# Third buffers for the split keys, packed token routing, and work moved into the attention, in a two-layer kernel on one Trainium2 core

## The reference, cut to what matters

```python
# layer 0
xn = layernorm(x)
ct_q, ct_kv = xn @ Wd_q + b, xn @ Wd_kv + b
query = heads(ct_q @ Wu_q) + heads(rope(ct_q @ Wq_r))      # 16 heads of 16
key   = heads(ct_kv @ Wu_k) + heads(rope(xn @ Wk_r))
s = softmax(query key' / scale) (ct_kv @ Wu_v) @ Wo + b
# g: 32 experts, each takes its 8 best tokens of a batch
probs = softmax(xn @ gate_w.T, over the 2048 tokens)
vals, idx = top_k(probs per expert, 8)
merged = sum_k xn[idx_k] * vals_k                          # one row per expert
o = gelu([merged, 1] @ w1) -> [.., 1] @ w2
g = zeros.at[idx].add(o * vals)                            # zero for most tokens
x = x + s * silu(g)
# layer 1: a state-space scan for s, a gated MLP for g
```

## Time and profile before

| | us |
|---|---|
| runs of the kernel before: median (lowest to highest) of 3 | 3020.09 (3019.51 to 3027.25) |
| the profiled execution, its own time | 3014.55 |
| its span, first to last instruction | 3012.9 |
| norm loop, until PE's first matmul of the key loop | 82.15 |
| key loop, until DVE's last `key_sum` | 233.5 |
| from there to the attention's first instruction | 49.5 |
| attention | 599.2 |
| scatter, from 964.3 | 47.5 |
| layer 1 | 2001.1 |

### The profile page before, as it was taken

How to read it: one execution, slowest core, us unless ns; L and a number is a source line. 1 busy time by engine, 2 the same in 40 slices (tenths; PEclk the granted TensorE clock), 3 DMA queues, 4 the chain that set the end, 5 groups by cost and what they waited for, 6 DMA issues and landing times.

```text
span 3012.9 us, 43961 instructions
## 1 busy us (share of the span) xinstructions
PE 2588.0 (86%) x13290; PEld 1488.0 (49%) x13290; DVE 2306.4 (77%) x2777; ACT 2027.6 (67%) x3268; POOL 2069.9 (69%) x650
## 2 busy tenths in 40 slices
PE   6776188888887769998999899999899899999987
PEld 2333033333333435564665555656556566566455
DVE  6577466556562269989889799898798888989995
ACT  3221146656564379878788698797787887978874
POOL 0454430000000179999999899999899999999996
PEclk9998579989998879999999999999999999999999
DMA  8335497767641123032132130321312303213210
GB/s 274 105 103 127 109 266 210 186 175 180 172 140 46 55 120 120 30 119 100 36 120 85 65 120 33 117 99 36 121 52 97 120 17 126 105 38 120 78 63 7
DMA packets 133934, 323.21 MB, mean 107 GB/s; under 512 B 13233, under 2 KB 89009, under 8 KB 117314
## 3 DMA queue, kind: packets, MB, share of 16 engines
q1 hardware_dynamic: 113186, 248.84, 26.7%
q0 software_dynamic: 19200, 70.73, 7.1%
q10 hardware_dynamic: 1312, 0.66, 0.1%
HBM read 277.12 MB, written 43.13 MB: 106 GB/s over the span
## 4 chain that ended last, share of the span: by engine, by line
PE 26%; issue 12%; POOL 12%; ACT 7%; DVE 7%; ACTq 1%; DVEq 1%; DMA 0%; POOLq 0%; SPq 0%
PE l_p_w L1995 11%; PE l_p_y L1987 6%; POOL l_st L1638 5%; PE l_p_w L2041 5%; DVE l_st L1457 4%; POOL l_st L1630 3%; PE l_p_w L2060 3%; ACT l_p_a L1716 2%; POOL keep_xg L1638 2%; DVE keep_xg L1457 1%; ACT L1791 1%; POOL l_dtu L1644 1%; ACT L1725 1%; DVE keep_xg L1466 1%; PE l_p_w L2017 1%
## 5 line engine op out<-in xcount | busy, mean ns | idle before, releaser
L1457 DVE TENSOR_TENSOR_SCAN l_st<-l_p_a,l_hl,l_st 128x512 f32<-128x512 f32 x768 | 931.6, 1265 | 112.1 <-ACT l_p_a L1716 93.0
L1638 POOL TENSOR_TENSOR l_st<-l_st,l_cs 128x2048 f32<-128x2048 f32 x192 | 868.6, 4541 | 4.1 <-ACT l_hl L1721 3.8
L1716 ACT ACTIVATE l_p_a<-l_dt,lw_a_neg 128x512 f32<-128x512 f32 x1024 | 666.1, 681 | 51.6 <-DVE keep_xg L1457 40.4
L1630 POOL TENSOR_TENSOR l_st<-l_bs,l_dtu 128x2048 f32<-128x2048 f32 x128 | 580.9, 4539 | 47.5 <-PE l_p_y L1987 44.2
L1987 PEld LDWEIGHTS l_p_y<-keep_ident,l_st 128*128 128x128 f32 x3072 | 353.8, 144 | 136.9 <-POOL l_st L1638 74.8
L1987 PE MATMUL l_p_y<-keep_ident,l_st 128*128 128x128 f32 x3072 | 382.4, 281 | 42.9 <-POOL l_st L1638 42.9
L977 ACT ACTIVATE a_pr<-a_p_s 128x512 f32<-128x512 f32 x512 | 284.8, 596 | 163.9 <-PE a_p_s L1043 145.7
L901 DVE TENSOR_REDUCE a_mpart<-a_p_m 128x1 f32<-128x512 f32 x512 | 315.2, 683 | 98.2 <-PE a_p_m L1008 96.5
L1457 DVE TENSOR_TENSOR_SCAN keep_xg<-l_p_a,l_hl,keep_xg 128x512 f32<-128x512 f32 x256 | 314.8, 1267 | 2.3 <-DVE keep_xg L1466 1.9
L1638 POOL TENSOR_TENSOR keep_xg<-keep_xg,l_cs 128x2048 f32<-128x2048 f32 x64 | 290.7, 4542 | 11.0 <-ACT l_hl L1721 11.0
L1043 PE MATMUL a_p_s<-a_qst,kx 99*128 99x256 bf16 x1024 | 206.7, 292 | 73.6 <-ACT a_pr L977 54.8
(11 more groups left out here) (225 smaller groups left out, 3920.1 us busy)
## 6 DMA issues: line engine op xcount, KB each, us to landing
a_w<-in_w_dram POOLq DMA_DIRECT2D x64, 1024.0 KB, 12.0
l_bs<-s_bc SPq DMA_DIRECT2D x64, 1024.0 KB, 4.7
l_cs<-s_bc SPq DMA_DIRECT2D x64, 1024.0 KB, 4.9
keep_share<-s_x SPq DMA_DIRECT2D x32, 512.0 KB, 4.4
s_kp<-t_kp SPq DMA_DIRECT2D x96, 128.0 KB
kx<-s_kp SPq DMA_DIRECT2D x16, 768.0 KB, 11.8
s_vp<-t_vo SPq DMA_DIRECT2D x16, 544.0 KB
a_vg<-s_vp SPq DMA_DIRECT2D x16, 544.0 KB, 11.7
```

The source lines that it names most:

```text
L1457: eng.tensor_tensor_scan(st[k % NG][:, n, :], p_a[:, n, :], st[k % NG][:, n, :], hl[:, k, n:n + 1], ALU.mult, ALU.add).then_inc(scan_ok, 1)
L1630: eng.tensor_tensor(st[n][:, :, :], bs[:, 4 * n:4 * n + 4, :], dtu[(k // NG) % 2][:, :].unsqueeze(1).broadcast_to([P, NG, TT]), ALU.mult). ...
L1638: eng.tensor_tensor(st[n][:, :, :], st[n][:, :, :], cs[:, 4 * n:4 * n + 4, :], ALU.mult).then_inc(cm_ok, 1)
L1716: eng.activation(p_a[:, n, :], dt[c % 2][:, :], ACT.Exp, scale=a_neg[:, c, m:m + 1]).then_inc(dA_ok, 1)
```

## The change

Its edits, in the order of the program:

1. Norm loop: x is no longer stored to `x1` from its buffers, and loads no longer wait for such stores. The buffers lie in `accT` now.
2. Key loop: three buffers `kp` and `vo`, two `k32`. They lie in a tensor `late` that outlives the stage and later holds the experts' `w2`.
3. The gather of `xg` is issued before `key_low(0)` instead of after `key_rest(1)`. The gather of the rotation's rows is issued in fours at tiles 4 and 6 instead of in twos at 4, 6, 8 and 9.
4. The routing steps run in tiles 0 to 12. ACT does `low(t+1)` before `high(t)`. The query parts are stored by SP at tile 13 and by ACT at tiles 13 and 14.
5. `share_of`, `rank_of` and `place` leave the loop. In the attention, `one_choice` does one column in two halves before each `take`, and the lists `rowb`, `rankb` and `rank` are loaded by SP after pass 3's loads (it issues those of passes 0 to 3 at once), and DVE waits for them in pass 1. `place` comes at the end.
6. The stage's end waits for the first two groups' keys and queries only, which it has loaded into `kst` and `q0`. The last stores of keys and values may land in the attention: SP waits for them before the loads of batch 1, POOL before its first `w2` load that overwrites them.
7. Attention: `identb` is made by ACT, and PE waits for it only at `transpose_max` of pass 0. x is copied to `x1` by eight 1 MB DMAs from DRAM to DRAM, one in each odd pass.
8. The result of an expert group uses a part of `hraw`, so `hidden_rows` waits for its store instead of `experts_out`.
9. Scatter: the eight rows' gather of `xg` is made again by POOL at its start, and DVE's first add of it waits for all eight.

On SP, in the stage's second part and at its end:

```diff
                 def keys_out(r):
-                    p = r % 2
+                    p = r % 3
...
+                def group_queries():
+                    eng.wait_ge(q_out, 16 * 6 * B)
+                    for hg in two:
+                        for g6, part in enumerate((0, 0, 0, 1, 1, 2)):
+                            eng.dma_start(q0[hg][g6 * 16:(g6 + 1) * 16, :, :].rearrange("r z t -> r (z t)"),
+                                          scr["qp"][0, hg, part * 64:(part + 1) * 64, :].rearrange("(r z) t -> r (z t)", z=4))\
+                               .then_inc(side, 16)
...
+                    if t == 13:
+                        store_queries(eng, 0)
                     if t in (10, 14):
                         group_keys((10, 14).index(t))
-                store_queries(eng, 0)
-                for p in two:
-                    eng.wait_ge(stored[p], STORES * (NT // 2))
-                for j in range(4):
-                    eng.wait_ge(x_out[j], 16 * (NT // 4))
-                eng.wait_ge(side, 16 * 9)
-                eng.wait_ge(q_out, 16 * 4 * B)
-                eng.wait_ge(q_out_g, 16 * 2 * B)
+                    if t == NT:
+                        group_queries()
+                eng.wait_ge(side, 16 * (1 + 2 * 3 + 2 * 6))
```

On DVE (`key_sum`, `values`; `high` on ACT changes as `values` does) and at the end of ACT's tile:

```diff
-                    wait(eng, r1_ok, t)
+                    wait(eng, r1_ok, t - 1)
...
-                    p = t % 2
+                    p = t % 3
                     eng.wait_ge(v_ok, t + 1)
-                    wait(eng, stored[p], t // 2 * STORES)
+                    wait(eng, stored[p], t // 3 * STORES)
...
                     if t in (13, 14):
-                        query_turned(2 * (t - 13) + 1)
-                eng.wait_ge(qsplit, 2)
-                eng.activation(qp[:, 1, :, :], qrest, ACT.Copy).then_inc(qsplit, 1)
+                        store_queries(eng, t - 12)
                 middle(NT - 1)
-                store_queries(eng, 1)
```

In the attention, on DVE, and on SP in `load`:

```diff
-                eng.tensor_copy(identb[:, :], ident[:, :]).then_inc(setup, 1)
...
+                def one_choice(g, b, hg):
+
+                    k = b * 2 + hg // 2
+                    wait(eng, shares, 6 * g)
+                    eng.tensor_copy(col[:, 0:1], gf[:, bass.ds(k, 1)])
+                    eng.tensor_copy(col[:, 1:2], vals[:, bass.ds(k, 1)]).then_inc(shares, 1)
+                    for h in two:
+                        cols = slice(h * TT, h * TT + TT)
+                        eng.wait_ge(shares, 6 * g + 2 * h + 1)
+                        if hg % 2 == 0:
+                            eng.tensor_scalar(found[:, :], rowb[:, cols], col[:, 0:1], col[:, 1:2], ALU.is_equal, ALU.mult).then_inc(shares, 1)
+                            eng.wait_ge(shares, 6 * g + 2 * h + 2)
+                            eng.tensor_tensor(share[:, cols], share[:, cols], found[:, :], ALU.add).then_inc(shares, 1)
+                        else:
+                            eng.scalar_tensor_tensor(found[:, :], rowb[:, cols], col[:, 0:1], rankb[:, cols], ALU.is_equal, ALU.mult)\
+                               .then_inc(shares, 1)
+                            eng.wait_ge(shares, 6 * g + 2 * h + 2)
+                            eng.tensor_reduce(part[:, h:h + 1], found[:, :], AX.X, ALU.max).then_inc(shares, 1)
...
-                    if not (isinstance(g, int) and g == 0):
-                        take(*prev(g, b, hg))
...
+                    if isinstance(g, int) and g == 0:
+                        return
+                    one_choice(*prev(g, b, hg))
+                    take(*prev(g, b, hg))
...
+                    if hg % 2:
+                        half = bass.ds(b * S + hg // 2 * (S // 2), S // 2)
+                        eng.dma_start(scr["x1"][half, :].rearrange("(p a) d -> p (a d)", p=P),
+                                      ins["x"][half, :].rearrange("(p a) d -> p (a d)", p=P)).then_inc(x1_out, 16)
```

In the scatter, on POOL:

```diff
+                    eng.indirect_dma_start(xg[:, k, :], None, ins["x"], bass.IndirectOffsetOnAxis(g8[:, k:k + 1], 0)).then_inc(xg_in, 16)
```

More of the change, by code:

```diff
@@ L802, in attention_stage @@
         w1 = sb("w1", [P, 4, KD, HID])
-        w2 = sb("w2", [P, 4, 8, D])
+        w2 = late[:, :].rearrange("p (j c d) -> p j c d", j=4, c=8)
+        rowb, rankb = (keep["xg"][:, 4 * i:4 * i + 4, :].rearrange("p k d -> p (k d)") for i in range(2))
+        found = sb("found", [P, TT])
+        part = sb("part", [P, 2])
+        rank, top, dup = (sb(n, [P, TOPK]) for n in ("rank", "top", "dup"))
+        col = sb("col", [P, 2])
         b1 = sb("b1", [P, NE, 8])
@@ L838, in prev, with all_stored @@
             return (g - 1, b if hg else b - 1, (hg - 1) % HG)
+        def all_stored(eng):
+            for j in range(3):
+                eng.wait_ge(stored[j], (6, 5, 5)[j] * STORES)
         def early(b, hg):
@@ L936, in step, with last @@
                         i.then_inc(hT_ok, 1)
[L937 to L940 removed]
+                    if isinstance(g, int) and g == 0:
+                        return
+                    one_choice(*prev(g, b, hg))
+                    take(*prev(g, b, hg))
+                def last():
+                    one_choice(G - 1, B - 1, HG - 1)
+                    place()
+                    take(G - 1, B - 1, HG - 1)
+                passes(eng, step, last)
             @block.scalar
             def _(eng):
+                eng.activation(identb[:, :], ident[:, :], ACT.Copy).then_inc(setup, 1)
                 def negT(g, b, hg):
```

312 lines of the change are left out of this document (150 added, 162 removed).

## The result

The changed kernel takes 2981.19 us, the median of four runs (2970.33 to 2985.24); the kernel before, run beside it, 3023.67 (3019.51 to 3027.87; four runs, three of them those of the section on the time before). The ratio is 0.9854, 95% interval 0.9822 to 0.9885: 42 us faster, where 80 were predicted and the range allowed 48 at least. The profiled execution took 2981.29 us (span 2979.6).

What follows compares the result with a forecast made beforehand. It took waits, not a full engine, to pace the key loop, and DMAs the norm loop. Terms -12 - 50 - 21 - 6 + 2 + 3 + 4 = -80 gave 2940 from the median; it predicted 2938 us, range 2905 to 2972.

Steps and rivals of the forecast that it cites:

- Norm loop: Norm loop: without the stores of x, DVE waits less for its loads; 12 us off, bounds 0 and 19.6.
- Key loop: Key loop: third buffers and less DVE work make PE the floor at 155 us; 183.5 instead of 233.5, 50 off.
- list of gathers, merge and turns: Key loop, on top of PE's floor: 9 us for gathers, 9.5 for the merge and two query turns.
- End of the stage: From the last `key_sum` to the attention: chain of 17 us, then SP's issues of 11; 28 instead of 49.5, 21 off.
- The stores stay the bound: Rival, key loop: stores still set the pace, so it gives 20 us instead of 50; 2968 us, chance 0.15.
- ACT's query stores hold the last tiles: Rival, last tiles of the key stage: two groups of ACT's stores cost 22 us more; 2960 us, chance 0.2.
- It changes nothing that counts: Rival: removed waits come back at the stage's end, which grows by 50 us; about 3016 us, chance 0.02.
- Attention: Attention: 6 us off for `identb`, 2 back for later weight loads, 3 added for the choices.
- `identb`: Attention's start: making it no longer holds PE; 6 us off.
- The choices: Attention, before `take`: a late `take` in odd passes is mostly hidden by ACT's table loads; 3 us added, bounds 0 and 50.
- The copies of x: Attention: 1 MB in two passes beside 8 MB of weights, which are loaded early; cost nothing.
- Scatter: Scatter's start: POOL's gathered rows land after DVE wants them; 4 us later, 0 to 8.

Runs made afterwards that it cites:

- b_x_copy_late: The kernel before, with only the copies of x moved to the attention: norm loop 77.5 us instead of 82.2, attention 597.7 instead of 599.0.
- b_no_choices: The kernel before, with shares and targets (47.0 us of DVE) left out of its key loop: key loop 223.6 us instead of 234.1.
- c_five: c_three with a tile's key parts stored by one DMA, partitions outermost, instead of six, and loaded by twelve instead of three: 2956.57 us, ratio to before 0.9781.
- c_three: The changed kernel with weights loaded later, two a tile, later query stores, short memsets, early lists, odd steps' choices in the wait: 2961.27 us, on another occasion 2955.55.

## Why the prediction was right and wrong

*Norm loop*, -12, measured -6.5 (b_x_copy_late: -4.7). The bounds held; the term was nearly twice too large. The weight loads, which I said can "still delay one load of x", stood ahead of a load for which DVE waited 10.2 us; a wait of 9.5 for the same tile is in the earlier trace rows, and I counted most of it to the copies. With the weights later, the loop took 71.5 us.

*Key loop*, -50, measured -45.6. The mechanism was right, since with two buffers in the changed kernel the loop's whole gain is gone. That the size is near is in part luck. I subtracted 47 us of DVE's work to reach a floor and did not ask what it is worth alone; with two buffers it is 10.5 (b_no_choices). And above PE's floor of 155 us the loop has 33.5 that my list of gathers, merge and turns, with 10 us added by estimate, names but does not explain: 14.0 to 16.9 us lie between the `key_sum` of tiles 2 to 5 and of tiles 8 to 10, and they stay in c_five, where `values` waits 0.8 us for stores. The rows of the gathers cost DVE 6.3 us, not 9. What holds those tiles no run took apart.

*End of the stage*, -21, measured +1.6: the step that failed. Its chain up to `key_low` took 25.9 us instead of 17, 11.56 of them ACT's wait for the stores of tile 12, and SP's part behind it 24.6 instead of 11. I counted SP's stores as instructions, "at about the 0.66 us of the earlier trace rows or less", and asked only whether ACT's query stores would hold ACT. What binds is the bytes behind them: a tile's key parts, 768 KB at 97 GB/s, are 8 us of drain, tiles 10 to 14 came 7.1 to 11.0 us apart, and 1.5 MB of queries are 16 us more. With the loop at its new pace there is little room for the queries, so their time comes back at the end (an estimate from these rates; the DMA row above, never under 2, agrees). No run gave the queries' stores the form of c_five as well, so that the end then shrinks is argued, not shown. The earlier trace rows had it: SP's six stores at 19.33 us beside ACT's eight at 21.36 and POOL's eight are 1.8 MB, 19 us at this rate. So had the earlier trace rows: the 7 us that I took for a landing were mostly the drain of the six parts issued before: of the 12.2 us from their first issue (275.51) to DVE's start, 8.1 are 768 KB at 97 GB/s (an estimate).

*The rivals.* "The stores stay the bound" came true by the sign that I had set (over 20 us; `values` stood 30.5), but at the end and not in the loop. Against it I held a DMA share of 0.41. That was the error in reading: a stage's mean share says nothing of a stream that can use four engines of sixteen, and such a stream is full at 0.27. "ACT's query stores hold the last tiles" named the right stage and half of the mechanism. ACT's first eight stores took 11.16 us, and behind them PE stood 4.66 for ACT's `low` and POOL 5.30 for `middle`:

```profile
246.84 11.16 ACTq L184 DMA_DIRECT2D s_qp<-t_wide  x8
...
259.73 3.66 PE L646 MATMUL t_p_b<-t_ckvT,t_w_uk 128*128 128x512 f32 x4 [4.66 <-ACT t_ckvT L476]
```

But ACT was slow because the same drain held its stores: four or eight more of them on ACT changed loop and end by 4 us, and in c_three, where the last eight stand behind ACT's last `middle`, the end is still 51.2.

In "It changes nothing that counts" an end longer by 50 us gives 3011 by the terms of the sum, not 3016.

*Attention*, -1, measured +7.5. `identb`, -6: PE's start gained 7 us and DVE's cast gave it back, since both were waits for POOL's memsets, which stayed. The choices, +3: measured 9.9. I said that a late `take` is hidden behind ACT's table loads; I had not followed DVE to the back edge of the loop, where PE stood 3.97 and 4.41 us for it, 8.4 of the 9.9. The copies of x, 0: right.

*Scatter*, +4, measured +0.7, inside the stage's spread: DVE waited 0.27 us for the gathered rows.

## What to carry to other kernels

A mean DMA share well under one does not clear the DMAs: look at the share while one kind of transfer runs alone, and if it stays at a round fraction of sixteen, look at the outermost dimension of that transfer before adding buffers or queues. When a loop is made faster, work that its waits used to hide comes back behind it; sum the bytes that the stage must drain and compare them with its new length. Put work that is moved into another loop inside a wait of that loop, and not between its last wait and the back edge.

## What was not expected of the hardware

Stores of key parts ran at 97 GB/s with 1 KB packets, 101 with 2 KB packets, 93 together with queries from a second queue, and 366 with the partitions outermost. A cast of 128x8 took 0.17 us or 7.00, by whether a memset of GpSimd was under way. Layer 1, untouched, moved by up to 18.6 us between executions, more than most single parts of this change.
